# An attention kernel whose row maxima reach Q by DMA instead of by a VectorE addition, with the work around its sixteen-sequence loop spread anew

## What is computed

```python
x = x + tanh(g_xattn[0]) * L0_xattn(layernorm(x), ctx)      # 16 heads of 8, keys and values from ctx
x = x + tanh(g_ffn[0])   * L0_ffn(layernorm(x))             # mixture of 16 experts, 4 chosen by a router
x = x + tanh(g_xattn[1]) * L1_xattn(layernorm(x), ctx)      # one head
x = x + tanh(g_ffn[1])   * L1_ffn(layernorm(x))             # butterfly MLP

def L0_xattn(x, ctx):                                       # per head h
    attn = softmax((x @ Wq.T + bq) @ (ctx @ Wk.T + bk).T * 8 ** -0.5)
    return concat_h(attn @ (ctx @ Wv.T + bv)) @ Wo.T + bo
```

## Time and profile before

| | us |
|---|---|
| median of 3 runs | 442.6 (442.52 to 453.13) |
| the profiled execution's own time | 445.52 |
| its span, first to last instruction | 443.7 |
| TensorE busy | 379.1 (85% of the span) |
| VectorE busy | 266.6 (60%) |
| GpSimd busy | 217.8 (49%) |
| ScalarE busy | 198.5 (45%) |
| mean granted TensorE clock | 0.892 |

### The profile page before, as it was taken

How to read it: one execution, slowest core, us unless ns; L and a number is a source line. 1 busy time by engine, 2 the same in 40 slices (tenths; PEclk the granted TensorE clock), 3 DMA queues, 4 the chain that set the end, 5 groups by cost and what they waited for, 6 DMA issues and landing times.

```text
span 443.7 us, 7130 instructions
## 1 busy us (share of the span) xinstructions
PE 379.1 (85%) x2654; PEld 246.4 (56%) x2654; DVE 266.6 (60%) x690; ACT 198.5 (45%) x372; POOL 217.8 (49%) x205
## 2 busy tenths in 40 slices
PE   5477679768978897999999999999999999578774
PEld 3244567556766674565555555555555565235554
DVE  8561566886668615856567857677666735552501
ACT  2142035533435434556545475464744457135222
POOL 6589899889794310744445424453343533400000
PEclk9696758985769657999999999999999999978999
DMA  8754333735441100000000000000000000000001
GB/s 254 116 109 114 95 118 125 129 108 141 107 133 49 52 0 1 1 1 1 0 0 1 1 1 1 0 0 2 0 0 0 2 0 0 1 0 1 24 25 47
DMA packets 7425, 19.55 MB, mean 44 GB/s; under 512 B 1208, under 2 KB 2396, under 8 KB 7264
## 3 DMA queue, kind: packets, MB, share of 16 engines
q0 software_dynamic: 3168, 11.54, 8.8%
q1 hardware_dynamic: 3504, 6.56, 6.7%
q10 hardware_dynamic: 720, 1.01, 0.7%
HBM read 16.02 MB, written 1.05 MB: 38 GB/s over the span
## 4 chain that ended last, share of the span: by engine, by line
PE 68%; DVE 13%; ACT 6%; DMA 6%; issue 3%; SPq 3%; POOL 1%; ACTq 0%; DVEq 0%
PE bank L843 12%; PE bank L710 7%; PE bank L828 6%; PE bank L829 6%; PE bank L830 6%; PE bank L835 5%; PE bank L736 5%; PE bank L952 4%; PE bank L963 3%; DMA rings<-qt_row 3%; DMA rows<-in_rows 3%; PE bank L717 2%; DVE nt L1078 2%; DVE pick_e L1072 2%; SPq L238 2%
## 5 line engine op out<-in xcount | busy, mean ns | idle before, releaser
L1279 DVE SCALAR_TENSOR_TENSOR rings<-rings,bank 128x512 f32<-128x512 f32 x64 | 43.9, 685 | 69.3 <-ACT rings L573 57.0
L400 POOL TENSOR_TENSOR rings<-rings 128x512 f32<-128x512 f32 x32 | 41.1, 1284 | 78.4 <-DVE rings L1282 69.9
L573 ACT ACTIVATE rings<-bank,b1c 128x512 f32<-128x512 f32 x64 | 44.1, 689 | 77.8 <-PE bank L830 77.4
L828 PE MATMUL bank<-xhl,w_hi 128*128 128x512 f32 x128 | 75.9, 593 | 0.0
L400 POOL TENSOR_TENSOR wide<-rings 128x512 f32<-128x512 f32 x32 | 41.8, 1306 | 47.5 <-DVE rings L1282 33.8
L1078 DVE TENSOR_REDUCE nt<-bank 128x4 f32<-128x480 f32 x64 | 40.0, 650 | 30.9 <-PE bank L717 30.9
L710 PE MATMUL bank<-rings,ks 32*120 32x128 f32 x512 | 49.0, 344 | 6.6 <-DVE nt L1078 5.1
L717 PE MATMUL bank<-ks,rings 32*128 32x120 f32 x512 | 47.6, 337 | 4.2 <-ACT qt_row L454 2.9
L829 PE MATMUL bank<-xhl,w_lo 128*128 128x512 f32 x128 | 51.1, 399 | 0.0
L830 PE MATMUL bank<-xhl,w_hi 128*128 128x512 f32 x128 | 51.0, 399 | 0.0
L710 PEld LDWEIGHTS bank<-rings,ks 32*120 32x120 f32 x512 | 41.7, 235 | 13.5 <-issue 11.0
(11 more groups left out here) (188 smaller groups left out, 684.6 us busy)
## 6 DMA issues: line engine op xcount, KB each, us to landing
bw<-in_flies POOLq DMA_DIRECT2D x18, 512.0 KB, 4.1
bw<-in_L_ffn_w POOLq DMA_DIRECT2D x4, 512.0 KB, 4.7
x_sb<-in_x SPq DMA_DIRECT2D x4, 256.0 KB, 7.7
rings<-qt_row SPq DMA_DIRECT2D x16, 64.0 KB
x_sb<-in_L_ffn_w SPq DMA_DIRECT2D x1, 1024.0 KB, 4.9
out<-xr SPq DMA_DIRECT2D x4, 256.0 KB, 2.4
wide<-in_ctx ACTq DMA_DIRECT2D x4, 240.0 KB, 7.9
ks<-kt_row SPq DMA_DIRECT2D x16, 60.0 KB
```

The costliest lines, as they stand in the source:

```text
L400: pool.tensor_tensor(es[e % len(es)], eq[:, e % 2, :], ec[:, e % 2, :], ALU.mult).then_inc(s["m_s"], 1)
L573: act.activation(esg[:, e % 2, :], SB[1 + e % 2][:, :], ACT.Gelu_apprx_sigmoid, bias=b1c[:, 0, e:e + 1]).then_inc(s["m_sg"], 1)
L828: pe.matmul(bk[:, :], w1_hi[:, e, branch, :], low(g), start=True, stop=False)
L1279: dve.scalar_tensor_tensor(eq[:, j, :], esg[:, j, :], GELU_LIMIT, (PQ, PO)[j][:, :], ALU.min, ALU.mult).then_inc(s["m_eq"], 1)
```

## The change

- **Maxima by DMA.** `maxima` now writes 4 x 4 numbers a sequence into a packed `nt`; TensorE turns them into 16 rows; ScalarE copies these to `mxr` (`turned_max`, first in each pass of its loop); SP's `stack_max(b)` writes them by one DMA of 8 KB into row 8 of each row group of `qs`. The transposed scores read `qs` itself. `less_maxima` and `qm` are gone. Matmuls keep their 32 rows. `ks` has ones in row 8 alone.
- **Queries and keys** of every group have a buffer of their own, so ScalarE no longer waits for the stacking DMAs. SP stacks K of groups 2 and 3 after the maxima of sequences 4 and 8, Q after those of 5 and 9, with one more DMA that puts zeros back into the maxima's rows. `w2` is loaded after the maxima of sequence 2.
- **First norm** for sequences 0 to 3 and then for the other 12, instead of all 16 at once; group 0's x is the second load, before the second half of the weights.
- **Values' bias.** Values leave PSUM without bias, by ScalarE's copies instead of VectorE's additions. Since softmax rows sum to one, the bias goes through Wo into the output's bias: one matmul with `bvb` (L0's bias broadcast by GpSimd), one VectorE operation (`row_bias`). The bias of L1's values is added on GpSimd during mixture 0 (`values1`).
- **Moved.** To GpSimd: the output bias on x (`xr`, after the splits of w1), `b1c`. To ScalarE: `pick_e`, in one operation at the start. The chunk biases of the butterfly (`ubs`) go behind the splits; the last `LATE` = 4 of the 18 butterfly stages, `up_bias_stages` and `values1` go between the products of mixture 0, `turn_down` to e = 14.
- **Second norm in halves** of 8 sequences instead of 12 and 4; group 0's norm and router run one or two passes earlier; `turn_gates(0)` stands after `up(0, 0)` and no longer after `project(15)`.

```diff
             def stack_q(g):
                 for i in range(HG):
                     sp.dma_start(qs[32 * i:32 * i + HD, g % 2, :, :],
-                                 qt_row[32 * i:32 * i + 32, g % 2, :]
+                                 q_rows[g][32 * i:32 * i + 32, :]
+                                 ).then_inc(s[f"qs_ld{g % 2}"], 16)
+                if g >= 2:
+                    sp.dma_start(qs[HD:P:32, g % 2, :, :], qs[HD + 1:P:32, g % 2, :, :]
                                  ).then_inc(s[f"qs_ld{g % 2}"], 16)
...
+            sp.wait_ge(s["qs_zero"], 1)
+            sp.wait_ge(s["qt_rdy"], 1)
+            stack_q(0)
+            sp.wait_ge(s["kt_rdy"], 2)
+            stack_k(1)
+            sp.wait_ge(s["qt_rdy"], 2)
+            stack_q(1)
+            def stack_max(b):
+                sp.wait_ge(s["mxr_rdy"], b + 1)
+                sp.dma_start(qs[HD:P:32, (b // GB) % 2, :, b % GB * P:(b % GB + 1) * P], mxr[:, b % 2, :]
+                             ).then_inc(s[f"mx_ld{b % 2}"], 16)
+            for b in range(NB):
+                stack_max(b)
+                g = b // GB + 1
+                if b == 2:
+                    sp.wait_ge(s["xr_rdy"], G)
+                    sp.dma_start(w2_sb[:, :, :], a["L0_ffn_w2"]).then_inc(s["ld_w2"], 16)
+                if b % GB == 0 and 2 <= g < G:
+                    sp.wait_ge(s["kt_rdy"], g + 1)
+                    sp.wait_ge(s["st_mm"], (g - 1) * GB * HG)
+                    stack_k(g)
+                if b % GB == 1 and 2 <= g < G:
+                    sp.wait_ge(s["qt_rdy"], g + 1)
+                    stack_q(g)
...
-            inverse_root(1, NB, False)
-            for g in range(G):
-                pool.wait_ge(s[f"ld_x{g}"], 16)
+            inverse_root(1, GB, False)
+            pool.wait_ge(s["ld_kb"], 16)
+            pool.tensor_copy(bvb[:, :], bcol[:, CV0:CV0 + 1].to_broadcast([P, P])).then_inc(s["bvb_rdy"], 1)
+            inverse_root(2, NB - GB, False)
             fetch(0)
             fetch(1)
-            pool.wait_ge(s["ld_ub"], 16 * 2)
...
+            pool.wait_ge(s["bo_rdy"], 1)
+            for g in range(G):
+                rows_ = slice(g * GB, (g + 1) * GB)
+                pool.tensor_tensor(xr[:, rows_, :], x_sb[:, rows_, :],
+                                   bcast[:, BO, :].unsqueeze(1).to_broadcast([P, GB, D]), ALU.add).then_inc(s["xr_rdy"], 1)
...
+                    if first(g) and e < 3 * LATE:
+                        stage(2 * STAGES - LATE + e // 3, e % 3)
+                    if first(g) and e == 3 * LATE:
+                        pool.tensor_copy(bft[0:1, 0:1], bfly[0:1, STAGES % 2, 0:1]).then_inc(s["bf_rdy"], 1)
+                        pool.wait_ge(s["bf_rdy"], 1)
+                        up_bias_stages()
+                    if first(g) and e >= 3 * LATE:
+                        values1(e - 3 * LATE)
+                    if e == E - 2 and first(g):
+                        inverse_root(4, HALF, True)
...
+            def turned_max(b):
+                act.wait_ge(s["nt_turned"], b + 1)
+                need(act, f"mx_ld{b % 2}", 16 * (b // 2))
+                act.activation(mxr[:, b % 2, :], TP[0:HG * HR, 0:P], ACT.Copy).then_inc(s["mxr_rdy"], 1)
...
             act.wait_ge(s["consts"], 1)
+            turned_max(0)
             spread_values(0)
             for b in range(NB + 2):
+                if b + 1 < NB:
+                    turned_max(b + 1)
                 if b < NB:
                     exps(b, 0)
                     exps(b, 1)
...
                     i, mc, tc = rows_of(b)
-                    pe.wait_ge(s["ntq_rdy"], b + 1)
+                    pe.wait_ge(s[f"mx_ld{b % 2}"], 16 * (b // 2 + 1))
                     need(pe, "exp_rdy", b * HG + 2 * half - 1)
                 if ahead < NB:
                     ia, ma, ta = rows_of(ahead)
                     if ahead % GB == 0 and half == 0:
                         pe.wait_ge(s[f"ks_ld{ia}"], 16 * HG * (ahead // (2 * GB) + 1))
-                        pe.wait_ge(s[f"qs_ld{ia}"], 16 * HG * (ahead // (2 * GB) + 1))
+                        pe.wait_ge(s[f"qs_ld{ia}"], 16 * (HG * (ahead // (2 * GB) + 1) + ahead // (2 * GB)))
                     need(pe, "nt_rdy", ahead * HG + 2 * half - 1)
                 for r in range(HR):
                     for j in range(2):
                         if 0 <= b < NB:
                             gg = 2 * half + j
                             mm = pe.matmul(turned_bank(b, gg)[0:M, r * P:(r + 1) * P], ks[32 * gg:32 * gg + 32, i, r, mc],
-                                           qm[32 * gg:32 * gg + 32, b % 2, r, :], start=True, stop=True)
+                                           qs[32 * gg:32 * gg + 32, i, r, tc], start=True, stop=True)
                             if r == HR - 1:
                                 mm.then_inc(s["st_mm"], 1)
                         if ahead < NB:
@@ -722,7 +783,7 @@
             def turn_max(b):
                 pe.wait_ge(s["nt_rdy"], (b + 1) * HG)
                 need(pe, "x1_rdy", b - 3)
-                pe.transpose(TP[:, 0:P], nt[:, :, :].rearrange("p g c -> p (g c)"), ident[:, :]).then_inc(s["nt_turned"], 1)
+                pe.transpose(TP[0:HG * HR, 0:P], nt[:, b % 2, :, :].rearrange("p g c -> p (g c)"), ident[:, :]).then_inc(s["nt_turned"], 1)
             def values(b):
...
             phase(-2, 0)
-            keys(3)
+            queries(2)
+            both_values(3)
+            turn_rows0(3)
+            queries(3)
+            pe.wait_ge(s["k1_rdy"], G)
+            pe.wait_ge(s["bvb_rdy"], 1)
+            pe.matmul(bank[5][:, 0:P], bvb[:, :], wt[:, WO0, :], start=True, stop=True).then_inc(s["bo_mm"], 1)
+            pe.wait_ge(s["qt_rdy"], G)
             phase(-2, 1)
-            both_values(3)
             phase(-1, 0)
             pe.wait_ge(s["v_rdy"], 2 * G)
             turn_max(0)
...
+                    pe.wait_ge(s["us_rdy"], 1)
+                    pe.matmul(bank[2][:, 0:HC], ubs[:, 1, :], ident[0:HC, 0:HC], start=True, stop=True
+                              ).then_inc(s["ub_turned"], 1)
                 if b >= 2:
                     turn_attn(b - 2)
+                if b == NB - 2:
+                    turn_normed(0)
                 phase(b, 1)
...
                     if first(g) and e == 0:
                         up(g, 0)
+                        turn_gates(0)
                         turn_attn(NB - 1)
                         up(g, 1)
                         project(NB - 1)
-                        turn_gates(0)
                     if not first(g) or e >= 2:
                         up(g, e)
...
+            def row_bias():
+                dve.wait_ge(s["ld_small"], 16)
+                dve.wait_ge(s["tanh_rdy"], 1)
+                own.then_wait(dve.tensor_scalar(bcast[:, BO, :], bcast[:, BO, :], tg[:, 0:1], None, ALU.mult))
+                dve.wait_ge(s["bo_mm"], 1)
+                dve.scalar_tensor_tensor(bcast[:, BO, :], bank[5][:, 0:P], tg[:, 0:1], bcast[:, BO, :],
+                                         ALU.mult, ALU.add).then_inc(s["bo_rdy"], 1)
             def maxima(b, n):
                 dve.wait_ge(s["s_mm"], b * HG + n + 1)
-                dve.tensor_reduce(nt[:, OF[n], HD:HD + HR], score_bank(b, n)[:, 0:HR * M].rearrange("p (r m) -> p r m", r=HR),
+                dve.tensor_reduce(nt[:, b % 2, OF[n], :], score_bank(b, n)[:, 0:HR * M].rearrange("p (r m) -> p r m", r=HR),
                                   AX.X, ALU.max, negate=True).then_inc(s["nt_rdy"], 1)
-            def less_maxima(b):
-                dve.wait_ge(s["nt_turned"], b + 1)
-                dve.tensor_tensor(qm[:, b % 2, :, :], qs[:, (b // GB) % 2, :, b % GB * P:(b % GB + 1) * P],
-                                  TP[:, 0:P].unsqueeze(1).to_broadcast([P, HR, P]), ALU.add
-                                  ).then_inc(s["ntq_rdy"], 1)
             def weighted(b):
...
                 if b >= 2:
                     weighted(b - 2)
-                if b + 1 < NB:
-                    less_maxima(b + 1)
                 if b + 2 < NB:
                     for n in range(HG - 1):
                         maxima(b + 2, n)
-                if b == NB - 2:
-                    refined(2, NB - GB, rr[:, :, 0:NB - GB], 2)
+                if b == NB - 3:
+                    refined(3, HALF, rr[:, :, 0:HALF], 2)
                     norm_rows(0)
+                if b == NB - 1:
+                    router_top(0)
+                if b == NB - 1:
+                    dve.wait_ge(s["ub_turned"], 1)
+                    dve.tensor_copy(ubx[:, 0, :], bank[2][:, 0:HC]).then_inc(s["ub_rdy"], 1)
                 if b == NB:
-                    router_top(0)
-                if b == NB + 1:
                     router_chosen(0)
...
                     own.wait()
-                    variances(NB - GB, stats[:, 0:NB - GB, :], mean[:, 0:NB - GB], True)
+                    variances(HALF, stats[:, 0:HALF, :], mean[:, 0:HALF], True)
...
```

296 lines of the change are left out of this document (134 added, 162 removed).

## The result

The changed kernel takes **450.0 us** (median of 4 runs, 447.7 to 451.2), the kernel before beside it 442.6. The ratio is 1.019, 95% interval 1.011 to 1.028; a second series gave 1.015 (1.005 to 1.025). So it is slower by 1.5 to 2%, and the forecast of 429.3 was wrong in sign. Both kernels were therefore profiled a second time.

The account below looks back on a forecast made before the run. TensorE was taken as the bound from 175 us on; in the attention loop it lost time to VectorE's maxima and a halved clock. Start -4.3, loop -6.3 and router -2.7 gave -13.3: 429.3 against 442.6, eight-in-ten range 414 to 448.

Parts of the forecast that it names:

- TensorE uses a product three experts later, so 0: Mixture 0: GpSimd's added butterfly work is covered because products are used three experts later; cost 0.
- the norm's VectorE work moves one pass earlier, with its 2 us: End of attention and start of the mixture: the norm's VectorE work, 2 us, comes one pass earlier.
- the loop's -6.3: Attention loop: 95.3 us (80.7 + 3 + 6.6 + 5) against 101.6 before, a gain of 6.3 us.
- TensorE's own 80.7 us: Loop without VectorE waits: three periods at 8.03 us less 2.3, and twelve at 4.91, 80.7 us.
- The DMA's two terms: Loop: 3 us exposed by the maxima's small DMAs in ten sequences, 6.6 us behind the stacks of groups 2 and 3.
- the 3.2 taken: Loop: assumed 3.2 us for a maxima DMA from issue to landing, hidden up to 3.0 at full clock.
- the 4 that the prediction names as a sign of being wrong: Loop: a landing time of the small DMAs over 4 us would show the forecast wrong.
- The 5 us for one fall of the clock: Loop: waits of about 2 us cause one clock fall, ten us of work at half speed, costing 5 us.
- a DMA that sets every sequence: Rival, 15%: butterfly fetches delay small DMAs to 4.7 us, nearly all loop periods run at half clock, 452 us.
- The start: Before the loop: earlier group 0 norm and unblocked queries put `turn_max(0)` at 42 instead of 46.5 us, -4.3.
- Router and gates: Start of the mixture: router one pass earlier, waits of 2.01 and 0.68 us for gates vanish, -2.7.
- End of attention: The 20 us after `turn_max(15)` were left as they are.

Follow-up runs that it names:

- e1: The changed kernel with its last four butterfly stages moved from mixture 0 to ahead of it, behind group 0's remainders: 444.0 us, ratio 1.008.
- e2: The changed kernel with its last four butterfly stages left out and nothing in their place: 438.8 us, ratio 0.998.
- e3: The kernel before with only its last four butterfly stages put into mixture 0 and the turn of the down weights at expert 14: 445.5 us, ratio 1.007.
- f1: The changed kernel with the second half's inverse root and refinement back in mixture 0: 445.4 us, ratio 1.011.
- f3: The changed kernel with two pauses of GpSimd at the first half's variances and norm in the loop: 441.2 us, ratio 0.989.
- g3: The changed kernel with both pauses, second half's norm in mixture 0, late stages split between behind the first gates and six experts of mixture 0: 440.8 us, ratio 0.999.
- h1: The changed kernel with both pauses, second half's norm in mixture 0, late stages spread over experts of all mixtures without small VectorE operations: 424.0 us, ratio 0.962.
- f4: The kernel before without any of its eighteen butterfly stages: 422.8 us, ratio 0.959.
- e4: The changed kernel without any of its eighteen butterfly stages: 421.8 us, ratio 0.960.
- f2: The changed kernel without the maxima's DMA per sequence; TensorE waits for ScalarE's copy and maxima are never subtracted: 444.9 us, ratio 1.004.
- h2: The changed kernel without the late stages, its loop stages fetching weights but computing nothing: 428.1 us, ratio 0.964.
- h3: The changed kernel without the late stages, its loop stages computing on the first two fetches' weights without fetches of their own: 426.4 us, ratio 0.969.

## Why the prediction was wrong, step by step

**The step that failed first: "TensorE uses a product three experts later, so 0".** I counted what GpSimd's late stages do to GpSimd's own queue, 8.7 of 10.2 us, and for the products that count held: one of them was late, by 0.4 us. Two things I did not count. The stages hold up VectorE, and the products' lead doesn't hide a late VectorE, whose `eq` and router stand directly ahead of TensorE: 3.2 us. And the turn of the down weights, at expert 14, waits for the last stage itself: 1.5 us. It cost 5.2 us in mixture 0 (e1, e2: 49.5 us without it; e3: the same edit makes the kernel before slower).

**The second: "the norm's VectorE work moves one pass earlier, with its 2 us".** I followed the first half and left out the second, `refined(4)`, which moved later, from mixture 0 to the head of mixture 1. There the first rows of the cross-attention, the router and a turn that needs both are waiting: 4.3 us of idle TensorE (2.6 to 2.9 without the late stages), a fall of the clock, 4.6 to 5.9 us in all (f1: 53.9 without it). The first half fared no better in the loop: moved beside the butterfly, its instructions took up to 2.95 us for 0.17 and cost a wait of 6.3; the two pauses give 3 to 6 us of the loop back (f3, g3, h1).

**The third, and by its size the largest: the loop's -6.3 was 0.** The forecast of 95.3 us for the changed loop was met (95.7, 94.9). What it was taken from, and why it should gain, were both wrong. The waits for VectorE's maxima I put down to VectorE's own list, to the additions and the casts that the change removes. Without the butterfly the kernel before has a loop of 81.8 us with all of them in place, and 3.5 us waited by the turns of the maxima instead of 9.9 (f4); the changed one has 81.2 (e4). So they are worth about half a microsecond there; what made them dear was the butterfly beside them, and the change left that in the loop. And 101.6 is the kernel before at a granted clock of 0.76; its second execution has 94.9 at 0.87, with nearly the same waits, while I applied the difference to a median: 15 of the 25 executions beside e1 took 436.9 to 443.2 us. The profile's 445.5 against a median of 442.6 was a hint of only 3 us, as the rest of that execution was a good one.

**The loop's forecast was right in sum, less so in parts.** TensorE's own 80.7 us looks like e4's 81.2, but by luck: that has 2.8 us of waits for DMA and 7.4 for maxima in it, and its first three periods take 17.8 us instead of 21.8. The DMA's two terms were 3 and 6.6; its waits were 8.0. Those at sequences 5, 6, 9 and 10, behind the stacks, were 2.98, 0.78, 2.39 and 0.45: 6.60 in all. Landing took at most 3.4 us for sequence 0 (issued at 44.44, used at 47.88) and 3.2 for sequence 13 (123.92, 127.14), about the 3.2 taken, but 4.7 to 5.5 at the four sequences behind the stacks (the longest 71.81, 77.33), over the 4 that the prediction names as a sign of being wrong. But these waits could not be had back: without the DMA (f2) other transfers and VectorE fill the same places. The 5 us for one fall of the clock covers, by chance, what the norm cost. The fixed cost of 2.0 us that the prediction cites from the Trainium skill (page "DMA: Bandwidth & Descriptors", section "Anatomy of one DMA") stands there for DMAs that GpSimd issues; these are SP's, and in the changed kernel and h2, where TensorE waited for one, it was 3.1 us or more from issue to use.

**The start**: 1.7 to 3.0 us for the 4.3 forecast. The first scores waited 4.04 us (2.96 in the second execution) for the stack of Q, which I had taken to be in time:

```profile
30.47 1.96 PE L778 MATMUL bank<-ks,rings 32*128 32x120 f32 x16 [4.04 <-DMA rings<-qt_row]
```

**Router and gates**: -2.7, and 13.2 to 10.3 and 10.6 measured: right. **End of attention**: 0, and 20.3 against 17.7 and 23.0, by the clock (0.69 and 0.50) in either direction: right on average, by luck.

**The rivals.** Their outcome "slower" had 13%, for a DMA that sets every sequence; it came to pass by another way. That rival's own sign, nearly all periods at half clock, is absent: the changed loop has 0.84 and 0.82. The rule of the Trainium skill (page "DMA: Bandwidth & Descriptors", section "Queues, rings and completion order"), that a semaphore's write waits for an engine's earlier writes of any queue, was given as a tendency; h2 and h3 agree with its direction, the small DMAs are waited for 8.2 us with the fetches and 2.8 without, but do not show that this is the way it comes about.

In sum, from the second pair of profiles: start -1.9, loop 0.0, end of attention +2.7 (clock), router -2.6, mixtures +5.3 and +4.6, the rest -0.2: +7.9 us, which is 445.8 against 437.8.

## What to carry to other kernels

GpSimd's idle time is not free where VectorE makes many short operations with SBUF operands: before moving GpSimd work, list VectorE's instructions in the new place and allow for some of them to last one to five GpSimd instructions (1.2 to 6.3 us here), then ask who waits for them. The same holds the other way round: before removing a long VectorE instruction, ask whether it is long by itself. Put such work where VectorE reads PSUM or has slack, as the slots of h1 do; the same twelve operations cost 5.4 us in one place and no more than 0.4 us a mixture in the others. And before a stage's time is compared, take it from two executions: a stage whose clock moves differs by 5 to 7 us on its own.

## What the runs showed of the hardware that I had not expected

- A VectorE instruction of 0.83 us was held over five consecutive GpSimd instructions, 6.28 us; it was not served between them.
- Work that nothing waits for in the loop, the butterfly, costs 19 us of 442 in the kernel before. Its loop is 13.1 us longer with it (94.9 and 81.8), the changed kernel's 13.6, of which fetches alone make 6.8 and operations alone 4.4; the granted clock of the loop is 0.91 in e4 and 0.88 and 0.87 in h2 and h3.
- One wait of 3.7 us in the dense part of the program was followed by some 15 us near half clock (g3), while waits of 1.05 and 1.59 us in mixture 0 of the changed kernel left the granted clock at 1.00. The length of a wait alone does not decide it: in mixture 0 of e3 one of 1.47 us lies in ten microseconds at 0.83.
